# Where the gathered rows of a routed mixture of experts are split into f16 halves: behind the transposes, or ahead of them

## The reference, cut to what matters

```
xn = layernorm(x)
out = x + attention(xn) + shared_ffn(xn) + routed_ffn(xn)
# routed_ffn: 8 experts, each token goes to its 2 best
gu  = x @ w_gate_up[e]                 # 512 -> 2 * 256
act = silu(gu[:256]) * gu[256:]
y   = act @ w_down[e]                  # 256 -> 512, times the token's combine weight
```

## Time and profile before

| | us |
|---|---|
| runs shown | 1427.99, 1428.18, 1429.99 |
| median | 1428.18 |
| the profiled execution | 1427.74 |
| its span | 1426.0 |

### The profile page before, as it was taken

One profiled execution on the slowest core, in us unless ns is written; L12 is line 12 of the kernel. 1 busy time (PEld: TensorE's weight loads), 2 busy tenths in 40 slices (PEclk: granted clock), 3 DMA queues, 4 the chain that ended last, 5 costly groups with the idle time before them and its releaser, 6 DMA issues. The chain is left out here.

```text
span 1426.0 us, 30118 instructions
## 1 busy us (share of the span) xinstructions
PE 1313.9 (92%) x10714; PEld 914.2 (64%) x10715; DVE 746.9 (52%) x1679; ACT 519.4 (36%) x1033; POOL 438.9 (31%) x391
## 2 busy tenths in 40 slices
PE   1599999999999986999999899999999979999998
PEld 1467776677766763777777555555555547777775
DVE  4478878787787866863333333333333313333323
ACT  3444444444444434332223244444444421111111
POOL 0333444334433331035430112122122132444433
PEclk9699999999999997999999999999999989999999
DMA  5224423344333443544432433333433341454333
GB/s 170 93 71 139 161 109 107 129 148 150 107 113 131 165 138 133 168 116 105 89 89 89 84 103 112 118 111 110 118 110 111 118 163 40 177 181 149 132 134 119
DMA packets 94526, 174.94 MB, mean 123 GB/s; under 512 B 21505, under 2 KB 27777, under 8 KB 94465
## 3 DMA queue, kind: packets, MB, share of 16 engines
q1 hardware_dynamic: 79008, 136.49, 28.4%
q0 software_dynamic: 13248, 36.78, 9.4%
q10 hardware_dynamic: 2208, 0.82, 0.2%
HBM read 117.28 MB, written 56.77 MB: 122 GB/s over the span
## 5 line engine op out<-in xcount | busy, mean ns | idle before, releaser
L1270 PE MATMUL gu<-xT,WG 128*128 128x256 f16 x3072 | 350.9, 275 | 21.8 <-DVE WD L1557 11.4
L1270 PEld LDWEIGHTS gu<-xT,WG 128*128 128x128 f16 x3072 | 303.0, 99 | 73.4 <-DVE WD L1557 12.1
L1281 PE MATMUL rgu<-WG,xh 128*128 x876 | 213.6, 380 | 5.4 <-issue 5.4
L1696 DVE SCALAR_TENSOR_TENSOR actv<-gu,up_inv,sg 128x512 f32<-128x512 f32 x64 | 48.0, 751 | 252.6 <-ACT sg L1533 252.4
L1251 POOL DMA_INDIRECT xg<-xn_dram,idx x76 | 71.9, 945 | 344.6 <-DVE idx L1246 324.2
L1533 ACT ACTIVATE sg<-gu,gate_inv 128x512 f32<-128x512 f32 x64 | 43.9, 687 | 318.0 <-PE gu L1270 318.0
L1288 PE MATMUL yp<-WD,ah 128*128 128x512 f16 x512 | 152.3, 379 | 1.2 <-DVE al L1701 1.2
L1281 PEld LDWEIGHTS rgu<-WG,xh 128*128 128x128 f16 x876 | 85.6, 98 | 95.0 <-issue 10.8
L655 PE MATMUL ring<-hh,qkvT 128*128 128x256 f16 x512 | 116.3, 275 | 6.0 <-DVE hl L973 6.0
L655 PE MATMUL ring<-hl,qkvT 128*128 128x256 f16 x512 | 116.2, 275 | 0.0
L1948 DVE TENSOR_TENSOR alr<-rat,ahr 128x256 f16<-128x256 f32 x72 | 30.6, 425 | 160.6 <-ACT ahr L1914 160.6
(11 more groups left out here) (240 smaller groups left out, 2246.3 us busy)
## 6 DMA issues: line engine op xcount, KB each, us to landing
y_dram<-ysb SPq DMA_DIRECT2D x72, 256.0 KB, 3.1
xl<-in_L_attn_x SPq DMA_DIRECT2D x16, 512.0 KB, 4.4
xn_dram<-xn SPq DMA_DIRECT2D x16, 512.0 KB, 6.4
wraw<-in_L_ffn_w_gate_up SPq DMA_DIRECT2D x16, 512.0 KB, 6.7
xT_dram<-x SPq DMA_DIRECT2D x16, 512.0 KB, 2.8
xr<-in_L_attn_x SPq DMA_DIRECT2D x16, 512.0 KB, 5.7
x_dram<-x SPq DMA_DIRECT2D x32, 256.0 KB, 2.1
xT<-xT_dram SPq DMA_DIRECT2D x16, 512.0 KB, 6.6
```

The source lines that it names most:

```text
L1270: ins = pe.matmul(gu[:, h, f * tokens:(f + 1) * tokens], w[:, kk, b, a0:a0 + P], x[:, kk, a], start=(kk == 0 and (a, b) == PASSES[0]), sto ...
L1281: ins = pe.matmul(gu[bank][:], x(kk, a), w[:, 0, kk, b, :], start=(i == 0), stop=(i == len(done) - 1))
L1696: v.scalar_tensor_tensor(out=actv[:, g % 2], in0=gu[g % 2][:, 1].rearrange("p (f t) -> p f t", f=FT), scalar=up_inv[:, 1:2], in1=sg[:], op ...
```

## The change: the split comes before the transposes

In `routed()`, ACT rounds the gathered f32 rows to f16 (`high_part`), POOL subtracts that from the rows and writes the remainder as f16 (`low_part`), and TensorE then turns both halves: eight f16 blocks of 128 x 128 against an f16 identity, into an f16 PSUM tile. ACT and DVE only copy the two turned halves out; `x_low` no longer reads what `x_high` wrote, and waits for the transposes alone. The factor X_SCALE is taken into the layer norm's reciprocal root in `attention`, so that `xn` is stored already scaled, and the scale leaves the copies. Gathers run five tiles ahead instead of four, behind the subtraction on POOL. `ident16` is kept for the whole kernel, and `ysb` takes a place in `raw`.

```diff
-AHEAD = 4
+AHEAD = 6
...
-                act.activation(sd[:, par], ve[:, par], ACT.Sqrt).then_inc(S["sd_ready"], 1)
+                act.activation(sd[:, par], ve[:, par], ACT.Sqrt, scale=X_SCALE ** -2).then_inc(S["sd_ready"], 1)
...
-                act.activation(xnT[:, 2 * i:2 * i + 2, :], bank[:].rearrange("p (k t) -> p k t", k=2), ACT.Copy,
-                               scale=X_SCALE
+                act.activation(xnT[:, 2 * i:2 * i + 2, :], bank[:].rearrange("p (k t) -> p k t", k=2), ACT.Copy
                                ).then_inc(S["xnT_ready"], 1)
...
+                xsp = sb(c, "xsp", [P, 2, 2, DIM], F16)
...
-                ysb = sb(c, "ysb", [P, 2, DIM])
+                ysb = raw[:, 0, 0:2]
...
-                xt = c.enter_context(nc.psum_tensor("xt", [P, KT, P], F32))
+                xt = c.enter_context(nc.psum_tensor("xt", [P, 2, 2 * KT, P], F16))
...
+                def later(q, par, tiles):
+                    return q + (par + tiles) // 2, (par + tiles) % 2
...
                 @block.gpsimd
                 def _(pool):
-                    for par in range(2):
-                        pool.wait_ge(S["xt_full"], par + 1)
-                        gather(pool, 1, par, S["pool_passed"])
+                    def low_part(q, par):
+                        r = 2 * q + par
+                        pool.wait_ge(S["high_ready"], r + 1)
+                        pool.tensor_tensor(xsp[:, par, 1], xg[:, par], xsp[:, par, 0], ALU.subtract
+                                           ).then_inc(S["low_ready"], 1)
+                        pool.wait_ge(S["low_ready"], r + 1)
+                        gather(pool, *later(q, par, 2), S["pool_passed"])
+
+                    for r in range(3):
+                        low_part(r // 2, r % 2)
 
                     def step(q, par, first):
-                        pool.wait_ge(S["xt_full"], 2 * q + par + 3)
-                        gather(pool, q + 2, par, S["pool_passed"])
+                        low_part(*later(q, par, 3))
...
                 @block.tensor
                     def turn(q, par):
-                        pe.wait_ge(xg_in[par], 16 * (q + 1))
-                        pe.wait_ge(S["xl_ready"], 2 * q + par)
-                        for kk in range(KT):
-                            ins = pe.transpose(xt[:, kk, :], xg[:, par, kk * P:(kk + 1) * P], ident[:])
+                        r = 2 * q + par
+                        pe.wait_ge(S["low_ready"], r + 1)
+                        pe.wait_ge(S["xh_ready"], r)
+                        pe.wait_ge(S["xl_ready"], r)
+                        for a in range(2):
+                            for kk in range(KT):
+                                ins = pe.transpose(xt[:, a, kk, :], xsp[:, par, a, kk * P:(kk + 1) * P], ident16[:])
                         ins.then_inc(S["xt_full"], 1)
...
                         own, nxt = places[-2:]
+                        pe.wait_ge(S["xh_ready"], r + 2)
                         pe.wait_ge(S["xl_ready"], r + 2)
...
                 @block.scalar
-                        act.activation(xh[:, par, 0], xt[:], ACT.Copy, scale=X_SCALE).then_inc(S["xh_ready"], 1)
+                        act.activation(xh[:, par, 0], xt[:, 0, 0:KT], ACT.Copy).then_inc(S["xh_ready"], 1)
+
+                    def high_part(q, par):
+                        r = 2 * q + par
+                        act.wait_ge(xg_in[par], 16 * (q + 1))
+                        if not (isinstance(r, int) and r < 2):
+                            act.wait_ge(S["xt_full"], r - 1)
+                        act.activation(xsp[:, par, 0], xg[:, par], ACT.Copy).then_inc(S["high_ready"], 1)
...
+                    high_part(0, 0)
+                    high_part(0, 1)
                     x_high(0, 0)
+                    high_part(1, 0)
                     x_high(0, 1)
...
                         x_high(q + 1, par)
+                        high_part(*later(q, par, 3))
...
                 @block.vector
-                        v.wait_ge(S["xh_ready"], r + 1)
-                        v.scalar_tensor_tensor(out=xh[:, par, 1], in0=xt[:], scalar=X_SCALE, in1=xh[:, par, 0],
-                                               op0=ALU.mult, op1=ALU.subtract).then_inc(S["xl_ready"], 1)
+                        v.wait_ge(S["xt_full"], r + 1)
+                        v.tensor_copy(xh[:, par, 1], xt[:, 1, 0:KT]).then_inc(S["xl_ready"], 1)
...
-                    for par in range(2):
-                        v.wait_ge(xg_in[par], 16)
-                        index(v, 1, par)
-                        x_low(0, par)
+                    next_index(1, 0)
+                    next_index(1, 1)
+                    x_low(0, 0)
+                    next_index(2, 0)
+                    x_low(0, 1)
...
-                        v.wait_ge(xg_in[par], 16 * (q + 2))
-                        index(v, q + 2, par)
+                        next_index(*later(q, par, 5))
```

More of the change, by code:

```diff
@@ L139, in build @@
         ones = sb(kept, "ones", [P, P])
+        ident16 = sb(kept, "ident16", [P, P], F16)
         logits = sb(kept, "logits", [P, B, NCH, E])
@@ L170, in build @@
         alpha = sb(attn, "alpha", [P, 2])
-        ident16 = sb(attn, "ident16", [P, P], F16)
         ounit = sb(attn, "ounit", [P, 1])
@@ L1205, in experts @@
 def experts(nc, sb, sem, k):
-    ident, ones, logits, wmax = k["ident"], k["ones"], k["logits"], k["wmax"]
+    ident, ident16, ones, logits, wmax = k["ident"], k["ident16"], k["ones"], k["logits"], k["wmax"]
     x1_steps, out_steps, xT_dram, xn_dram, y_dram, slot_dram = (
@@ L1791, in routed @@
                 yp = [c.enter_context(nc.psum_tensor(f"ryp{i}", [P, DIM], F32)) for i in range(2)]
-                xt = c.enter_context(nc.psum_tensor("xt", [P, KT, P], F32))
-                names = "gu_full act_ready sg_ready at_full ah_ready al_ready y_full y_ready xt_full xh_ready xl_ready cw_ready pool_passed"
+                xt = c.enter_context(nc.psum_tensor("xt", [P, 2, 2 * KT, P], F16))
+                names = ("gu_full act_ready sg_ready at_full ah_ready al_ready y_full y_ready xt_full high_ready low_ready "
+                         "xh_ready xl_ready cw_ready pool_passed")
                 S = {x: sem(c, "r_" + x) for x in names.split()}
@@ L1822, in _ @@
                 def _(pool):
-                    for par in range(2):
-                        pool.wait_ge(S["xt_full"], par + 1)
-                        gather(pool, 1, par, S["pool_passed"])
+                    def low_part(q, par):
[7 more added lines that the diff above has]
+                        low_part(r // 2, r % 2)
                     def step(q, par, first):
-                        pool.wait_ge(S["xt_full"], 2 * q + par + 3)
-                        gather(pool, q + 2, par, S["pool_passed"])
+                        low_part(*later(q, par, 3))
                     run_steps(pool, step)
-                    for par in range(2):
-                        pool.wait_ge(xg_in[par], 16 * (SLOT_TILES // 2 + 2))
+                    pool.wait_ge(xg_in[0], 16 * (SLOT_TILES // 2 + 3))
+                    pool.wait_ge(xg_in[1], 16 * (SLOT_TILES // 2 + 2))
                 @block.tensor
@@ L1852, in _ @@
                     turn(0, 1)
+                    pe.wait_ge(S["xh_ready"], 1)
                     pe.wait_ge(S["xl_ready"], 1)
@@ L1929, in x_low, with next_index @@
                         r = 2 * q + par
-                        v.wait_ge(S["xh_ready"], r + 1)
-                        v.scalar_tensor_tensor(out=xh[:, par, 1], in0=xt[:], scalar=X_SCALE, in1=xh[:, par, 0],
-                                               op0=ALU.mult, op1=ALU.subtract).then_inc(S["xl_ready"], 1)
+                        v.wait_ge(S["xt_full"], r + 1)
+                        v.tensor_copy(xh[:, par, 1], xt[:, 1, 0:KT]).then_inc(S["xl_ready"], 1)
+                    def next_index(q, par):
+                        v.wait_ge(xg_in[par], 16 * q)
+                        index(v, q, par)
                     weight(0, 0)
                     weight(0, 1)
-                    for par in range(2):
-                        v.wait_ge(xg_in[par], 16)
-                        index(v, 1, par)
-                        x_low(0, par)
+                    next_index(1, 0)
[3 more added lines that the diff above has]
+                    x_low(0, 1)
                     def step(q, par, first):
```

## The result

The changed kernel takes 1432.53 us (median of 9 runs, 1430.61 to 1434.41), the kernel before, run beside it, 1427.86 (9 runs, 1426.58 to 1429.99): 4.7 us more, a ratio of 1.0029 [1.0019, 1.0038]. The forecast was 1432.4, +4.2. The profiled execution took 1433.65, its span is 1431.9.

A forecast was written before the change was run, and what follows sets the result against it. TensorE, busy for 92% of the span, was taken as the bound, with uncovered chains at both ends of `routed()`. Terms 0.4 + 0.8 + 2.2 + 0.8 = +4.2 us on 1428.18 gave 1432.4 us, range 1428.5 to 1438.

The forecast's parts named there:

- Transposes: TensorE, 72 tiles: eight f16 blocks take 0.445 us against 0.44 for four f32 ones, +0.4 us in all.
- faster rival: TensorE's `turn`: a transpose is paid by its weight load alone, 0.032 us each, -9.5 us in all; chance 0.07.
- dearer one: TensorE's `turn`: f16 transposes cost more than f16 matmuls, 0.083 us each, +20 us with the other terms; chance 0.08.
- Turns of the loop: TensorE's sequencer where its loop turns: one more wait costs +0.1 us, eight times, +0.8 us.
- The start: Start of `routed()`: POOL's gather 2 before its second subtraction delays the second `turn` and first gate/up matmuls, +2.2 us.
- The end: End of `routed()`: POOL issues the last gather later, behind rounding and subtraction, before its drain and the barrier, +0.8 us.
- ACT, POOL and DVE in the loop: Tile loop: rounding, subtraction and copies on these engines fit within the 4.54 us step; nothing counted.
- everything else: Scale moved in `attention`, longer index tables, `ident16` and `ysb` moved in memory: counted at nothing.
- POOL as the bound: POOL in the loop: a subtraction over 2.6 us delays `turn` in every tile; at 3.0 it costs 29 us; chance 0.04.
- rival of hidden ends: Both ends of `routed()`: start at its lower bound, end costs nothing, +2.1 us remain, 1430.3; chance 0.18.

The follow-up runs named there:

- e_double: Changed kernel with every f16 transpose made twice, 16 instead of 8 a tile: 1462.55 us, 1.0228 of the kernel before.
- a_trim: Changed kernel without any surplus work for slot tiles 72 and later: 2.8 us slower than `b_trim2`.
- b_trim2: `b_trim` run again, beside the other trimmed kernels: 10.2 us below the kernel before, ratio 0.9928.
- e_order: Changed kernel with both first POOL subtractions ahead of the gathers of tiles 2 and 3: 1432.93 us, 1.0027 of the kernel before.
- a_early: Changed kernel with tiles 0 and 1 split on ACT and POOL before the barrier: 1430.68 us, 1.0012 of the kernel before.
- b_trim: Kernel before without any surplus gather, turning, gate/up matmul, split or weighting for tiles 72 on: 1419.18 us, 0.9928 of the kernel before.
- e_notail: Changed kernel without gathers, indices or waits for tiles 72 to 76: 1427.62 us, 0.9994 of the kernel before.
- b_notail: Kernel before without the four gathers for slot tiles 72 to 75, other surplus work kept: gains 7.6 us.
- e_rest: Kernel before with only the small edits (scale folded, longer index tables, `ident16` and `ysb` moved): 1429.32 us, 0.9998 of the kernel before.
- e_warm: Changed kernel with 12 unused matmuls on TensorE around the first turns of `routed()`: 1431.94 us, 1.0022 of the kernel before.
- b_fill: `b_trim` with unused matmuls on TensorE in the gaps at both ends (16, 4 and 24): 1420.46 us, 0.9935 of the kernel before.

## Why the prediction was right

*Transposes: forecast +0.4, measured +0.7.* The price was right: 0.45 us for eight blocks against 0.445 reckoned from the earlier trace rows, and the step grew from 4.540 to 4.550 us (median of 71 steps in each trace). By line, with the count, the duration (ns, min/median/max) and the starts:

```profile
L1855 PE MATMUL xt<-ident,xsp x592: 219/219/314, 817.2 to 1157.4; 128*128 128x128 f16 x198
```

`e_double` confirms it by another way, and `a_trim` less `b_trim2` leaves 0.6 for it and the turns of the loop. The faster rival (a block paid by its weight load) and the dearer one (f16 transposes slower than f16 matmuls) are both out: 16 blocks took 0.89 us, 0.056 each. That is also why the change gains nothing: twice the blocks at half the price each. By the 81 ns of the Trainium skill (page "TensorE: Matmul & The Clock Gate", section "Back-to-back issue gap") the eight would have taken 0.65 and the kernel some 14 us more, an estimate; the trace disagrees with it.

*Turns of the loop: forecast +0.8, measured +0.2.* This is the step that failed, with its mechanism. I took each added wait for one step of the sequencer. But in the trace the wait instruction of `L1879` carries two conditions, the waits for `xh_ready` and `xl_ready` together (the one of `L1863` before carried one), and the wait for `act_ready` rides on the register instruction behind it, as before. The added wait costs no step of its own. The gaps sum to 5.6 against 5.4 us.

*The start: forecast +2.2, measured +2.2.* The mechanism is shown twice: taking the gather from between the subtractions gives 1.2 back (`e_order`), and splitting ahead of the barrier gives all of it and more (`a_early`). The 2.2 holds against starts of the old order at 4.03 or 4.04 us, three of five traces; in the other two the first turning was quicker and the start at 3.53 or 3.54, 2.7 below the changed kernel's. The granted clock differs there: 0.81 on average in `b_trim` from 813.70 to 816.90, 0.50 in the kernel before from 813.84 to 817.40. So the term is known to half a microsecond only.

*The end: forecast +0.8, measured +1.2.* The subtraction by line:

```profile
L1831 POOL TENSOR_TENSOR xsp<-xg,xsp x75: 1153/1156/1162, 816.0 to 1158.9; 128x512 f16<-128x512 f32 x75
```

The subtraction takes 1.16 us, not the 1.07 of half the larger one, so part of its time does not shrink with the size. The gather is issued 0.93 us later against the last matmul, the landing adds 0.2 and the drain 0.08. `a_trim` and `b_trim2`, with a gap of 3.64 in both, show that the term goes with the surplus work. Taking out the surplus gathers alone is not enough: then the changed kernel has 6.48 (`e_notail`) and the kernel before 3.64 (`b_notail`), since POOL still makes its surplus subtractions and starts to drain at 1158.29, while in `b_notail` it starts at 1141.0.

*ACT, POOL and DVE in the loop, and everything else: forecast nothing, measured nothing.* The timeline of the tile and `e_rest` show it. POOL as the bound is out: it is busy for 2.1 us of 4.55, or 3.0 with the wait ahead of the gather.

*Not foreseen: the clock at the start.* In the changed kernel's two traces the first 18 gate/up matmuls take 5.68 and 5.70 us, against 5.00 before, with seven or eight of them at the lower clock. That is +0.7 in those executions. Whether it belongs to the change stays open: `e_rest` starts in the old order and took 6.26, `a_trim` starts in the new and took 5.07. One profile of each can't tell such a term from the scatter between executions.

The terms as measured are 2.2 + 0.7 + 0.2 + 1.2 = 4.3 us without the clock and 5.0 with it; the medians say 4.7 and 4.8. The forecast of 4.2 had 0.6 too much at the loop and 0.7 too little in transposes and end. The ends and the price of a block were right by their mechanism; that the sum came within 0.6 us is luck in part, since the 0.6 too much at the loop and the 0.7 too little elsewhere cancel. The rival of hidden ends fails on both: neither was hidden.

## What to carry to other kernels

Where an engine is busy throughout, read a replacement as count times pitch, and find the pitch in rows of the same type and shape: half the price for twice the count gains nothing. The rest of such a change is decided where nothing overlaps, at the barriers: follow there, on each engine, which instruction stands before the one that is waited for. And look at what a pipeline does past its last tile: gathers for tiles that nobody uses cost 7 us here, more than the whole change.

## What the runs showed of the hardware

- POOL's drain at the end of `routed()` took 5.77 us in the six traces without surplus gathers (in `e_notail` with no gather issued in the 20 us before it), and 6.10 in the kernel before and 6.18 in the changed one. In `b_trim` it ran beside the matmuls and cost nothing.
- An f16 block transposed into an f16 PSUM tile costs as much as an f16 matmul of as many columns, 0.056 us, its weight load included, at the granted clock 1.00; an f32 one 0.11.
- The time that the first matmuls of a block spend at the lower granted clock depends on more than the kernel's order: without filling the same 18 matmuls took 4.96 to 6.31 us over twelve traces (old order of the start 4.96, 5.00, 5.12, 5.15, 6.26; the changed kernel's 5.04, 5.07, 5.38, 5.68, 5.70; `a_early` 5.55, `e_order` 6.31). In `e_warm` and `b_fill`, where TensorE had filling in its gaps there, they took 4.05.
- Two waits that follow each other can be one instruction of the sequencer (`L1879`), so counting waits in the code overstates their cost.
